# Token-major layer norm for the feed-forward stage: statistics and whitening on VectorE, one split on GpSimd

## The reference

```python
def ffn_layer(x, g, bln, W1, b1, W2, b2):
    mu = x.mean(-1, keepdims=True)
    var = ((x - mu) ** 2).mean(-1, keepdims=True)
    xn = (x - mu) / jnp.sqrt(var + 1e-05) * g + bln
    hg = xn @ W1 + b1
    a, gate = jnp.split(hg, 2, -1)
    return a * jax.nn.gelu(gate, approximate=False) @ W2 + b2
for i in range(DEPTH):
    x = attn_layer(shift_tokens(x), Wqkv[i], q_scale[i], k_scale[i], Wo[i]) + x
    x = ffn_layer(shift_tokens(x), ln_g[i], ln_b[i], W1[i], b1[i], W2[i], b2[i]) + x
```

## Time and profile before

| what | value |
|---|---|
| median of 3 executions | 3221.99 us (3219.24 to 3224.43) |
| profiled execution, its own time | 3217.83 us |
| span of its trace | 3216.0 us |
| one iteration in the steady part | 63.83 us |
| of it, TensorE busy | 62.55 us |
| of it, VectorE / ScalarE / GpSimd busy | 55.54 / 50.19 / 53.60 us |

### The profile page before, as it was taken

One profiled execution on the slowest core, in us unless ns is written; L12 is line 12 of the kernel. 1 busy time (PEld: TensorE's weight loads), 2 busy tenths in 40 slices (PEclk: granted clock), 3 DMA queues, 4 the chain that ended last, 5 costly groups with the idle time before them and its releaser, 6 DMA issues.

```text
span 3216.0 us, 150706 instructions
## 1 busy us (share of the span) xinstructions
PE 3074.7 (96%) x63810; PEld 2604.6 (81%) x63810; DVE 2666.9 (83%) x4403; ACT 2428.2 (76%) x4920; POOL 2516.4 (78%) x2510
## 2 busy tenths in 40 slices
PE   5999999999999999999779999999999999999997
PEld 4888888888888888888668888888888888888886
DVE  3888888888888888888558888888888888888884
ACT  4777777777877777787537777777777778777874
POOL 5987887888788788787349878878887888888772
PEclk8999999999999999999879999999999999999998
DMA  2221222222222222221112222222212212222221
GB/s 84 76 61 49 76 64 54 70 67 54 64 71 56 64 66 60 67 66 52 32 25 80 60 52 74 62 53 71 68 52 67 72 52 68 62 61 54 56 51 38
DMA packets 117860, 195.45 MB, mean 61 GB/s; under 512 B 23756, under 2 KB 36552, under 8 KB 117192
## 3 DMA queue, kind: packets, MB, share of 16 engines
q1 hardware_dynamic: 117192, 185.82, 22.0%
HBM read 33.71 MB, written 1.05 MB: 11 GB/s over the span
## 4 chain that ended last, share of the span: by engine, by line
PE 78%; DVE 11%; issue 5%; POOL 2%; ACT 2%; DVEq 0%; DMA 0%; ACTq 0%; POOLq 0%; SPq 0%
PE of_ps L982 10%; PE tr L997 9%; PE s_ps L945 8%; PE tr L958 6%; PE tr L883 5%; PE qk_ps L883 4%; PE qk_ps L885 4%; PE qk_ps L884 4%; PE of_ps L1047 4%; PE tr L910 4%; PE tr L923 4%; DVE ss_floor L736 3%; PE tr L885 2%; PE tr L884 2%; DVE xs_lo L708 2%
## 5 line engine op out<-in xcount | busy, mean ns | idle before, releaser
L431 POOL TENSOR_TENSOR rotated<-rotated 128x1024 f32<-128x1024 f32 x384 | 916.6, 2387 | 23.7 <-DVE rotated L729 23.7
L458 POOL TENSOR_TENSOR rotated<-rotated,rn 128x1024 f32<-128x1024 f32 x384 | 731.1, 1904 | 30.1
L437 POOL TENSOR_TENSOR prob<-prob,rden 128x512 f32<-128x512 f32 x384 | 440.3, 1147 | 290.8 <-DVE rden L761 285.5
L537 ACT ACTIVATE sq<-qk_ps 128x1024 f32<-128x1024 f32 x384 | 393.2, 1024 | 265.5 <-PE qk_ps L885 193.8
L723 DVE TENSOR_TENSOR rotated<-qk_ps,rot 128x1024 f32<-128x1024 f32 x384 | 469.1, 1222 | 118.4 <-ACT sq L537 108.2
L729 DVE TENSOR_TENSOR rotated<-qk_ps,rot 128x512 f32<-128x512 f32 x768 | 490.7, 680 | 0.0
L736 DVE TENSOR_REDUCE ss_floor<-sq 128x16 f32<-128x1024 f32 x384 | 464.0, 1208 | 0.4
L997 PE MATMUL tr<-ot,wo 128*128 128x128 f32 x3072 | 410.3, 277 | 0.2 <-issue 0.2
L982 PE MATMUL of_ps<-pt,vs 64*64 64x32 f32 x12288 | 391.0, 222 | 8.0 <-DVE hid L793 2.2
L982 PEld LDWEIGHTS of_ps<-pt,vs 64*64 64x64 f32 x12288 | 325.7, 134 | 78.5 <-issue 48.7
L945 PEld LDWEIGHTS s_ps<-kt,qt 64*32 64x32 f32 x24576 | 268.4, 105 | 142.6 <-issue 142.2
(11 more groups left out here) (136 smaller groups left out, 7022.5 us busy)
## 6 DMA issues: line engine op xcount, KB each, us to landing
vs<-vn SPq DMA_DIRECT2D x384, 192.0 KB, 2.5
vs<-vtail SPq DMA_DIRECT2D x384, 64.0 KB, 2.0
vtail<-vn SPq DMA_DIRECT2D x384, 64.0 KB, 2.1
staging<-layer_wqkv_dram SPq DMA_DIRECT2D x72, 256.0 KB, 3.0
wo<-layer_wo_dram SPq DMA_DIRECT2D x12, 512.0 KB, 3.8
xs<-xa SPq DMA_DIRECT2D x48, 128.0 KB, 2.3
fs<-xa SPq DMA_DIRECT2D x48, 128.0 KB, 2.3
xs<-xa SPq DMA_DIRECT2D x48, 127.8 KB, 2.4
```

What stands on the lines that cost most here:

```text
L431: nc.gpsimd.tensor_tensor(rot_c[h], rot_c[h], rot_s[h], ALU.add).then_inc(rot_added, 1)
L437: nc.gpsimd.tensor_tensor(prob[h][:, :, :], prob[h][:, :, :], rden[h][:, :].unsqueeze(2).to_broadcast([P, 2 * PAIRS, KEYS]), ALU.mult).the ...
L458: nc.gpsimd.tensor_tensor(folded, folded, rn[:, :].unsqueeze(2).to_broadcast([P, 2 * UH, DH]), ALU.mult).then_inc(qkn_ready, 1)
```

## The change

The norm's statistics are taken with the tokens on the partitions. At the end of slot 3 TensorE transposes the four token tiles into `f_ps`; VectorE takes `bn_stats` of each in slot 4, joins them by `bn_aggr` after the rotations, and adds epsilon after the differences; GpSimd's power stands in slot 4, not 5. In slot 5 VectorE whitens the four tiles from PSUM (subtract the mean, multiply by the inverse deviation, both from SBUF, one value per partition) into `ftok`. At the end of slot 6 TensorE transposes back. In slot 7 ScalarE applies gain and bias and makes the high part, and GpSimd the low part.

```diff
-MEAN_AT, VAR_AT, SPREAD_AT, NORM_AT, GATED_AT, DOWN_AT, ADD_AT = 3, 4, 6, 7, 8, 9, 10
+TURN_AT, STATS_AT, WHITE_AT, BACK_AT, NORM_AT, GATED_AT, DOWN_AT, ADD_AT = 3, 4, 5, 6, 7, 8, 9, 10
...
+            def normed_low(it):
+                pool.wait_ge(fn_hi_ready, ONE + it + 1)
+                nc.gpsimd.tensor_tensor(fn_lo[:, :], fd[:, :], fn_hi[:, :].bitcast(F32), ALU.subtract).then_inc(fn_split, 1)
...
-            def centred(it):
-
-                act.wait_ge(fcen_ready, ONE + it + 1)
-                nc.scalar.activation(fsq[:, :].rearrange("p (a n) -> p a n", a=2), f_ps, ACT.Square).then_inc(fsq_ready, 1)
-                nc.scalar.activation(fd[:, :].rearrange("p (a n) -> p a n", a=2), f_ps, ACT.Copy).then_inc(fd_ready, 1)
-
-            def normed_high(it):
+            def normed(it):
                 l = it // SEQS % DEPTH
-                act.wait_ge(fn_ready, ONE + it + 1)
+                act.wait_ge(fback_ready, ONE + it + 1)
+                act.wait_ge(fn_split, ONE + it)
+                nc.scalar.activation(fd[:, :].rearrange("p (a n) -> p a n", a=2), f_ps, ACT.Identity,
+                                     scale=vecs[:, l, 0:1], bias=vecs[:, l, 1:2]).then_inc(fd_ready, 1)
+                act.wait_ge(fd_ready, ONE + it + 1)
                 act.wait_ge(gated_ps, ONE + 2 * NCH * it)
-                nc.scalar.activation(fn_hi[:, :], fd[:, :], ACT.Identity, bias=vecs[:, l, 1:2]).then_inc(fn_hi_ready, 1)
+                nc.scalar.activation(fn_hi[:, :], fd[:, :], ACT.Copy).then_inc(fn_hi_ready, 1)
...
+            def statistics(it):
+                dve.wait_ge(ftr_ready, ONE + it + 1)
+                for c in range(TPS):
+                    last = nc.vector.bn_stats(fstat[:, c, :], f_ps[:, c // 2, c % 2 * P:(c % 2 + 1) * P])
+                last.then_inc(fstat_ready, 1)
+
+            def moments(it):
+                dve.wait_ge(fstat_ready, it + 1)
+                for c in range(TPS):
+                    last = nc.vector.bn_aggr(fmoment[:, c, :], fstat[:, c, :])
+                last.then_inc(fmoment_ready, 1)
...
+            def whitened(it):
+                dve.wait_ge(frstd_ready, ONE + it + 1)
+                dve.wait_ge(fback_ready, ONE + it)
+                for c in range(TPS):
+                    last = nc.vector.tensor_scalar(ftok[:, c, :], f_ps[:, c // 2, c % 2 * P:(c % 2 + 1) * P],
+                                                   fmoment[:, c, 0:1], rstd[:, c:c + 1], ALU.subtract, ALU.mult)
+                last.then_inc(ftok_ready, 1)
...
-                if (it := ffn_of(p, n, VAR_AT + 1)) is not None:
-                    pe.wait_ge(fvar_ready, ONE + it + 1)
-                if (it := ffn_of(p, n, SPREAD_AT + 1)) is not None:
-                    pe.wait_ge(fn_ready, ONE + it + 1)
+                if (it := ffn_of(p, n, STATS_AT)) is not None:
+                    pe.wait_ge(fstat_ready, it + 1)
+                if (it := ffn_of(p, n, WHITE_AT)) is not None:
+                    pe.wait_ge(ftok_ready, ONE + it + 1)
+                if (it := ffn_of(p, n, NORM_AT + 1)) is not None:
+                    pe.wait_ge(fd_ready, ONE + it + 1)
...
-                for i in range(2):
-                    last = nc.tensor.matmul(f_ps[:, i, :], centre_mat[:, :], fs[:, i * HS:(i + 1) * HS], start=True, stop=True)
-                last.then_inc(fcen_ready, 1)
...
                 for c in range(TPS):
-                    last = nc.tensor.matmul(f_ps[:, 0, c:c + 1], fsq[:, c * P:(c + 1) * P], mean_mat[:, 0:1], start=True, stop=True)
-                last.then_inc(fvarp_ready, 1)
...
+                    last = nc.tensor.transpose(f_ps[:, c // 2, c % 2 * P:(c % 2 + 1) * P], fs[:, c * P:(c + 1) * P], ident[:, :])
+                last.then_inc(ftr_ready, 1)
...
+            def feature_major(it):
+                pe.wait_ge(ftok_ready, ONE + it + 1)
                 for c in range(TPS):
-                    last = nc.tensor.matmul(f_ps[:, c // 2, c % 2 * P:(c % 2 + 1) * P], rstd[:, c:c + 1].to_broadcast([P, P]), ident[:, :],
-                                            start=True, stop=True)
-                last.then_inc(frb_ready, 1)
+                    last = nc.tensor.transpose(f_ps[:, c // 2, c % 2 * P:(c % 2 + 1) * P], ftok[:, c, :], ident[:, :])
+                last.then_inc(fback_ready, 1)
```

More of the change, by code:

```diff
@@ L372, in _ @@
                         stage_tokens(p, it)
-                    if (it := ffn_of(p, n, MEAN_AT - 1)) is not None:
+                    if (it := ffn_of(p, n, TURN_AT - 1)) is not None:
                         shift_ffn(it)
@@ L391, in _ @@
         def _(pool):
-            for released in (rn_ready, rot_added, qkn_ready, probn_ready, w1_split, frstd_ready):
+            for released in (rn_ready, rot_added, qkn_ready, probn_ready, w1_split, frstd_ready, fn_split):
                 pool.sem_inc(released, ONE)
@@ L478, in _ @@
                         normalise(n + 1)
-                    if (it := ffn_of(p, n, VAR_AT + 1)) is not None:
-                        pool.wait_ge(fvar_ready, ONE + it + 1)
-                        nc.gpsimd.tensor_tensor(rstd[:, :], var[:, :], minus_half[:, 0:TPS], ALU.pow).then_inc(frstd_ready, 1)
+                    if (it := ffn_of(p, n, STATS_AT)) is not None:
+                        inverse_deviation(it)
+                    if (it := ffn_of(p, n, NORM_AT)) is not None:
+                        normed_low(it)
                     g, m = layer_slot(p, n)
@@ L811, in _ @@
                         tokens_low(it)
-                    if (it := ffn_of(p, n, VAR_AT + 1)) is not None:
-                        variance(it)
-                    if (it := ffn_of(p, n, SPREAD_AT + 1)) is not None:
-                        spread(it)
-                    if (it := ffn_of(p, n, NORM_AT + 1)) is not None:
-                        normed_low(it)
+                    if (it := ffn_of(p, n, STATS_AT)) is not None:
+                        statistics(it)
+                    if (it := ffn_of(p, n, WHITE_AT)) is not None:
+                        whitened(it)
                     if live(p, n + 2):
                         rotate(n + 2)
+                    if (it := ffn_of(p, n, STATS_AT)) is not None:
+                        moments(it)
                     if live(p, n):
@@ L822, in _ @@
                         differences(n)
+                    if (it := ffn_of(p, n, STATS_AT)) is not None:
+                        variance(it)
                     if live(p, n - 2):
@@ L1073, in _ @@
                         project_out(p, n - 2)
-                    if (it := ffn_of(p, n, MEAN_AT)) is not None:
-                        centre(it)
-                    if (it := ffn_of(p, n, VAR_AT)) is not None:
-                        variances(it)
-                    if (it := ffn_of(p, n, SPREAD_AT)) is not None:
-                        spread(it)
+                    if (it := ffn_of(p, n, TURN_AT)) is not None:
+                        token_major(it)
+                    if (it := ffn_of(p, n, BACK_AT)) is not None:
+                        feature_major(it)
                     if (it := ffn_of(p, n, GATED_AT)) is not None:
```

59 lines of the change are left out of this document (25 added, 34 removed).

## The result

The changed kernel took 3260.5 us (median of 4 executions, 3253.7 to 3261.5) where the kernel before took 3221.6 (3219.2 to 3224.4): a ratio of 1.0116, with a 95% interval of 1.0098 to 1.0133. It is slower by 39 us. The forecast was 3231, with 3260 as the upper end of its range; the median lies half a microsecond past that end.

A forecast was written before the change was run, and what follows sets the result against it. TensorE, busy 96% of the span, was taken as the bound, with VectorE close behind. Waits and transposes of 2.91 us against 2.72 saved gave 0.19 us more per iteration, 9 us in 48: 3231 us, range 3214 to 3260.

The forecast's parts named there:

- TensorE's saving: Per iteration TensorE loses 2.72 us of work and gains 0.88 us of transposes; alone, 1.84 us saved, 88 in 48.
- The wait in slot 4: TensorE waits 0.67 us at `weigh_values` for the four `bn_stats`, taken as 0.21 us from start to start.
- VectorE's short operations don't overlap: Rival: statistics and whitening each cost full busy time, 0.48 us more per iteration, 3254; chance 0.22 shared with dear statistics.
- a dear statistics pass: Rival: each `bn_stats` in slot 4 takes 0.34 us, 0.52 us more per iteration, 3256; chance 0.22 shared with no overlap.
- `bn_aggr` is hidden: In slot 4 four `bn_aggr`, 0.48 us, fit in the 0.49 us VectorE has before the row maxima.
- The wait in slot 5: TensorE waits 1.31 us for VectorE's four whitenings, taken as 0.26 us from start to start and 0.34 for the last.
- a saving in slot 7: L982 in slot 7 took 1.14 us against 1.06 because it waited for `fd`; that excess was counted as saved.
- Slot 8: TensorE waits 0.05 us for the scaled probabilities behind GpSimd's low part; nil at best, 0.55 if GpSimd is slowed.
- `var` is hidden in front of `xa`: VectorE's `var` costs nothing, since it stands ahead of `xa`, which waits for TensorE.
- The two waits don't bind: Rival: TensorE's whole saving comes through, 88 us less, 3134; chance 0.03.
- the lead reaches the stretch where VectorE is the bound: Rival: `fn_lo` leaving slot 8 helps slots 10 and 11 by up to 0.82 us, 39 us less, 3192; chance 0.05.

The follow-up runs named there:

- fill: Changed kernel with TensorE doing slot 5's key transposes three times over, same result, ahead of the wait for the whitened tiles: 3241.1 us, ratio 1.0062 to the kernel before.
- nowait5_tt: Changed kernel with the whitening replaced by a product of two SBUF operands and no TensorE wait for it in slot 5: 3259.8 us, ratio 1.0127 to the kernel before.
- nowait5: Changed kernel with the whitening reading an SBUF tile instead of PSUM and no TensorE wait for it in slot 5: 3259.0 us, ratio 1.0117 to the kernel before.
- w1_later: Changed kernel with GpSimd's split of the first feed-forward weight moved 3 slots later and its load 2 later: 3256.0 us, ratio 1.0108 to the kernel before.
- nowait4: Changed kernel with the statistics reading an SBUF tile and no TensorE wait for them in slot 4: 3273.7 us, ratio 1.0163 to the kernel before.
- both_first: Changed kernel with slot 5's whitening and slot 4's statistics placed ahead of VectorE's row sums, nothing left out: 3196.3 us, ratio 0.9922 to the kernel before.

## Why the prediction was right in kind and short in size

**TensorE's saving: right.** The forecast was busy time down by 85 us with the span about unchanged. It fell by 62.6, and what the lower clock took grew by (1 − 0.977) × 3259.8 − (1 − 0.983) × 3216.0 = 20 us: about 83 without that, the same as the 62.55 − 60.82 = 1.73 us of one iteration, 48 times.

**The wait in slot 4: right.** 0.60 us against 0.67, in all of 46 iterations, because `bn_stats` takes 0.19 from start to start and not 0.21. The rival "VectorE's short operations don't overlap" is out: an operation busy for 0.28 us lets the next start after 0.19. So is the rival of a dear statistics pass, and `bn_aggr` is hidden as worked out.

**The wait in slot 5: the term that was mis-sized.** 1.31 us were forecast and 1.53 measured, in an undisturbed iteration. The step was "I take 0.26 from start to start": it is 0.31, for the per-partition cost of 0.05 was put down once and the whitening reads two such values. Four of them are 0.2 us, 10 us in 48 iterations. The table by slot has the whole of the difference in this one: +0.72 in slot 5 and not +0.42.

**Small terms.** L1003 takes 1.14 us behind a wait and 1.06 without; the sum had that as a saving in slot 7 but not as a cost in slots 4 and 5 (0.08 us). Slot 8 is 0.12 us longer and not 0.05. Together the undisturbed iteration is 0.52 us longer than before and not 0.19: 25 us in 48 where 9 were forecast.

**What was in no term: the clock.** The falls cost some 20 us: fill takes 19 off, and layers of four iterations with no fall took 256.4 and 256.6 us, with one 257.4 to 258.5, and with three 260.2 and 260.3. The prediction read a granted clock of 1.00 in its one iteration and carried it over to a kernel whose TensorE idles for 1.3 us in one piece, where the longest idling in that iteration before was 0.65. None of its rows could have priced it, but the trace of before had a warning outside the steady part: TensorE idles for 1.88 us, and the clock behind it is 0.50.

```profile
131.17 1.11 PE L958 MATMUL tr<-ident,prob 128*128 128x128 f32 x4 [1.88 <-POOL prob L437]
...
132.00:134.00 2.00, 2.00 (x11) 2.00 (x10) 0.00 (x0) 1.61 (x3) 2.00 (x2) 0.50 0.37 80
```

The same stands at 1735.32, while an idling of 2.10 us at 1566.20 was followed by none. No bound was kept for it.

**What was in no term: the shared port.** The twelve held `var` make slot 5 0.6 us longer (8.72 against 8.11), 7 us in twelve. The prediction says "`var` is hidden in front of `xa`", by the 0.11 us of a `var` that read PSUM; the new one reads SBUF. The Trainium skill states it in "SBUF — State Buffer", section "Who interferes with whom": a VectorE operation whose source lies in SBUF and which uses both port pairs, as a `tensor_scalar` may, shares one pair with GpSimd, and whoever has it first blocks the other altogether. By that rule `var` waits for the end of L460, and the trace agrees (921.19 against 921.17); the same section has two SBUF inputs contend as well, with which nowait5_tt agrees, and leaves an operation with one source, in PSUM, alone: the whitening at 923.48 takes 1.33 us beside an L433 that began at 922.26 and lasts 2.35, half of what the SBUF form took in nowait5.

**The account.** From the first output projection of a pass to the last, the passes grew from 1502.4 to 1529.0 us and from 1501.2 to 1526.8, by 52 us together. Of them 48 iterations at 0.52 make 25 and the twelve held `var` 7. The 20 that are left go to the 16 falls, 1.2 us each if the one of twice the length counts double, and that is what fill took off. Not all of the 20 need be the clock's: TensorE idles for some tenths in slot 6 of some iterations with no releaser in the profile (slot 6 lasts 7.00 and not 6.50 at 352 us), and what that is stays open. The stretch between the two passes shrank from 101.8 to 95.6 us and the one behind the last output projection from 35.2 to 33.1, 8 us together, which gives the 43.8 of the spans; no run takes apart why. w1_later doesn't show what the held `var` costs by itself, since the wait that it removed came back at L977.

**What was luck.** That the change is slower was forecast for the right reason: 105 us of waiting outweigh 83 us of work. Without the falls and the held `var` the time would have been about 3221.6 + 25 − 8 = 3239 us, an estimate from the account above and slower all the same. That the range reached to the result is luck: its upper end was there for short operations that don't overlap (3254 to 3256), which the intervals of 0.19 us refute, and what brought the time there was in no term.

**The faster rivals.** "The two waits don't bind" is out by 105 us of waiting. That the lead reaches the stretch where VectorE is the bound didn't show: slots 9 and 10 are as long as before (slot 9 lasts 13.63 us in both).

## What to carry to other kernels

When work moves from the engine that is the bound to one that runs just behind it, look first at where the new work stands in that engine's queue: the same operations cost 39 us behind a row sum whose result wasn't needed yet and gave 18 to 25 ahead of it. Count every operand of a new short operation, and ask of each small VectorE operation with an SBUF source what GpSimd does at that time. A wait of over 1.5 us on TensorE may cost more than its length through the clock, so compare the granted clock of both traces before the waits are added up.

## What the runs showed of the hardware that was not expected

- TensorE's granted clock fell from 1.00 to 0.50 behind 16 of 46 waits of 1.52 to 2.2 us, with the engine busy before them at 1.00, and it took back some 1.7 us of full-speed time each (3.4 behind one). Behind the same length of wait it mostly did not: ten of 35 at 1.5 us, six of 11 at 2.1. Work of no use in the waits removed all 16 (fill). What decides between two alike waits no run here shows.
- A per-partition value in SBUF costs a VectorE operation over 128 columns from PSUM 0.06 us from start to start each: 0.19, 0.25, 0.31 (and 0.28, 0.34, 0.40 busy).
- `bn_stats` of 128 columns from PSUM is busy for 0.28 us, 0.19 from start to start; `bn_aggr` of six values 0.155 and 0.07.
- An operation over four elements per partition was stretched from 0.16 us to between 0.84 and 0.95 by GpSimd's work in SBUF, 12 times of 48, always at the same place of a layer. Where VectorE came to it earlier (nowait4, both_first), it was held in 46 of 48, mostly to 0.3 us and in twelve to 1.3.
